# The second norm's normalising, turns, projection and residual addition two steps sooner in the memory stage

## The reference, cut to what matters

```python
keys = (x @ Wk.T + bk).reshape(B, L, N_QUAT, 4)
keys = keys / jnp.maximum(knorm, NORM_EPS)
values = (x @ Wv.T + bv).reshape(B, L, N_QUAT, 4)
bound = quat_mul(values, keys)
memory = jnp.cumsum(bound, axis=1)
retrieved = quat_mul(memory, quat_conj(keys)).reshape(B, L, D)
retrieved = retrieved / jnp.sqrt(positions)[None, :, None]
normed = (retrieved - mu) / jnp.sqrt(var + LN_EPS) * ln_g + ln_b
return x + (normed @ Wo.T + bo)
```

## Time and profile before

| | us |
|---|---|
| median of three runs | 881.63 |
| profiled execution | 886.1 |
| its span, first to last instruction | 884.3 |
| PE busy | 759.0 (86%) |
| DVE busy | 639.8 (72%) |
| ACT busy | 463.6 (52%) |
| POOL busy | 479.7 (54%) |
| mean granted PE clock | 0.919 |

### The profile page before, as it was taken

One profiled execution on the slowest core, in us unless ns is written; L12 is line 12 of the kernel. 1 busy time (PEld: TensorE's weight loads), 2 busy tenths in 40 slices (PEclk: granted clock), 3 DMA queues, 4 the chain that ended last, 5 costly groups with the idle time before them and its releaser, 6 DMA issues.

```text
span 884.3 us, 14563 instructions
## 1 busy us (share of the span) xinstructions
PE 759.0 (86%) x3937; PEld 572.3 (65%) x3938; DVE 639.8 (72%) x1468; ACT 463.6 (52%) x927; POOL 479.7 (54%) x438
## 2 busy tenths in 40 slices
PE   5999999996488299943989997998989898989997
PEld 2444444553377299942878886777868686868785
DVE  3789999988364255534699996878786968787864
ACT  2455556652122177723466655665656565756553
POOL 2677777765036444432356663554655555555554
PEclk9999999998555599975899999899999999999999
DMA  5000000000392122211000003545546281909280
GB/s 184 0 1 1 0 1 0 0 2 0 47 371 93 45 62 64 69 39 48 18 20 1 1 1 82 114 99 109 121 85 146 60 171 37 189 23 193 49 165 12
DMA packets 36383, 60.14 MB, mean 68 GB/s; under 512 B 3568, under 2 KB 15472, under 8 KB 35680
## 3 DMA queue, kind: packets, MB, share of 16 engines
q1 hardware_dynamic: 34048, 54.73, 26.6%
q0 software_dynamic: 2272, 4.67, 1.6%
HBM read 51.11 MB, written 8.28 MB: 67 GB/s over the span
## 4 chain that ended last, share of the span: by engine, by line
PE 31%; issue 8%; POOL 7%; DVE 6%; ACT 2%; DMA 1%; POOLq 0%; SPq 0%; DVEq 0%; ACTq 0%
PE c_m L1496 3%; PE c_m L1498 3%; PE c_m L1497 3%; POOL d_hid_lo L2017 2%; PE c_v L1496 1%; PE c_k L1496 1%; PE c_o L1550 1%; PE c_k L1497 1%; PE c_k L1498 1%; POOL c_bound L1984 1%; PE c_o L1547 1%; PE c_o L1548 1%; POOL c_read L1990 1%; PE c_v L1498 1%; PE c_r L1550 1%
## 5 line engine op out<-in xcount | busy, mean ns | idle before, releaser
L2017 POOL TENSOR_TENSOR d_hid_lo<-c_bound,d_hid_hi 128x512 fp32r<-128x512 f32 x136 | 176.6, 1299 | 152.6 <-ACT d_hid_hi L1947 152.4
L1947 ACT ACTIVATE d_hid_hi<-c_bound 128x512 fp32r<-128x512 f32 x136 | 85.2, 626 | 49.8 <-DVE c_bound L1809 48.8
L576 POOL TENSOR_TENSOR a_rs<-a_r,a_state 128x512 f32<-128x512 f32 x64 | 75.2, 1186 | 29.9 <-DVE a_state L419 27.5
L419 DVE TENSOR_TENSOR_SCAN a_state<-a_decay,a_state,a_vb 128x512 f32<-128x512 f32 x64 | 81.2, 1269 | 0.0
L1076 POOL DMA_INDIRECT results<-b_y_row,b_result_row x39 | 37.5, 960 | 51.9 <-DVE b_y_row L999 35.3
L1496 PE MATMUL c_m<-d_x_hi,d_hi 128*128 128x512 f32 x136 | 56.3, 414 | 7.5 <-DVE c_bound L1809 7.5
L1800 DVE TENSOR_TENSOR c_m<-c_bound,c_m 128x512 f32<-128x512 f32 x64 | 44.3, 692 | 23.7 <-PE c_m L1498 17.4
L1800 DVE TENSOR_TENSOR c_v<-c_bound,c_v 128x512 f32<-128x512 f32 x64 | 44.3, 692 | 22.2 <-PE c_v L1498 16.7
L990 DVE TENSOR_TENSOR b_hidden<-b_h,b_b 128x512 f32<-128x512 f32 x39 | 27.0, 692 | 42.9 <-PE b_h L826 42.2
L1498 PE MATMUL c_m<-d_x_hi,d_lo 128*128 128x512 f32 x136 | 54.1, 398 | 0.0
L1497 PE MATMUL c_m<-d_x_lo,d_hi 128*128 128x512 f32 x136 | 54.1, 398 | 0.0
(11 more groups left out here) (305 smaller groups left out, 2181.2 us busy)
## 6 DMA issues: line engine op xcount, KB each, us to landing
d_w_wide<-pair_weights SPq DMA_DIRECT2D x64, 512.0 KB, 12.1
b_w<-in_w SPq DMA_DIRECT2D x2, 2048.0 KB
d_w_wide<-in_moe SPq DMA_DIRECT2D x3, 1088.0 KB
b_xin<-rows_in SPq DMA_DIRECT2D x39, 64.5 KB
d_w_wide<-results SPq DMA_DIRECT2D x8, 256.0 KB
out<-c_read SPq DMA_DIRECT2D x8, 256.0 KB, 2.2
a_weights<-in_mixing SPq DMA_DIRECT2D x1, 901.0 KB
shape_consts<-in_consts SPq DMA_DIRECT2D x1, 744.0 KB, 5.0
```

Source lines behind the costliest of these rows:

```text
L419: dve.tensor_tensor_scan(state[:, j, seq_cols(h, 1)], decay[:, h, :], vb[j % 3][:, :], first, ALU.mult, ALU.add).then_inc(scan_ready, 1)
L576: pool.tensor_tensor(rs[:, j, :], rr[:, h, :], state[:, j, seq_cols(h, 0)], ALU.mult).then_inc(rs_ready, 1)
L1947: act.activation(hid_hi[:, n % HALVES, :], hidden[:, r, :], ACT.Copy).then_inc(hi_ready, 1)
L2017: pool.tensor_tensor(hid_lo[:, n % HALVES, :], hidden[:, r, :], hid_hi[:, n % HALVES, :].bitcast(F32), ALU.subtract).then_inc(lo_ready, 1)
```

## The change

In the tail, ACT's two halves of the normalising go from steps 6 and 7 to 4 and 5 and `normed_t` from 9 to 7; PE's turns go from step 8 to 6 and the projection from 11 to 9; DVE's addition goes from step 13 to 11. Within a step the tail comes first, so in step 4 ACT meets the normalising and its wait for `shift2` before copy 1, and in step 11 DVE meets the addition before `lo`. No instruction is added, dropped or altered, and POOL's and SP's orders stay.

```diff
                 def tail(i, h, step):
-                    if step == 8:
+                    if step == 6:
                         pe.wait_ge(normed_ready, i + 1)
...
-                    if step == 11:
+                    if step == 9:
                         pe.wait_ge(normedt_ready, i + 1)
                         need(pe, x_ready, i)
                         project(bank_o, "bo", "wo", normed_t).then_inc(wo_out, 1)
...
-                    if step == 13:
+                    if step == 11:
                         dve.wait_ge(wo_out, i + 1)
                         dve.wait_ge(kept_ready, i + 1)
...
-                    if step in (6, 7):
-                        if step == 6:
+                    if step in (4, 5):
+                        if step == 4:
                             act.wait_ge(shift2_ready, i + 1)
                             need(act, normedt_out, i)
-                        for s in (0, 1) if step == 6 else (2, 3):
+                        for s in (0, 1) if step == 4 else (2, 3):
...
-                        if step == 7:
+                        if step == 5:
                             a.then_inc(normed_ready, 1)
-                    if step == 9:
+                    if step == 7:
                         act.wait_ge(normedt_out, i + 1)
                         need(act, wo_out, i)
```

## The result

The changed kernel takes 892.26 us (median of 4 runs, 891.38 to 892.57) against 880.63 us (879.02 to 881.84): 1.32% slower, ratio 1.0132 with the 95% interval 1.011 to 1.0153. Forecast was 891.9.

The account below looks back on a forecast made before the run. DVE and PE were taken as both nearly full in a memory-stage body of 14.9 us. Terms 0.9 + 6.5 + 2.06 + 1.70 - 0.88 gave +10.3 on 881.6: 891.9 us, range 885 to 895.5.

Parts of the forecast that it names:

- `normed` can't start sooner: On ACT, normed already starts 0.04 us after shift2 ends, so standing sooner in the order can't start it sooner.
- Bodies 1 to 6: Memory-stage delays from got to got: body 1 +0.9 us, bodies 2 to 5 +1.63 each, body 6 +2.06.
- Copy 3 at Z+4.07: ACT's last memory copy ends 4.07 us after Z, shift2's end: 1.52 us later than before, bounds 0.98 and 2.1.
- `memory_n` +0.77: DVE's memory_n, which had 0.75 us of slack, starts 0.77 us later, 4.11 us after shift2 ends.
- first sum +0.41: PE's first sum of read comes 0.41 us later, 5.26 us after shift2 ends.
- `got` at Z+10.74: DVE's got starts 10.74 us after shift2 ends, not 9.11: +1.63 us a body.
- The port: DVE and GpSimd instructions exclude each other, first issued first; lo now waits for GpSimd's second read, delaying real and got.
- Rival 1: Port waits don't grow, second lo precedes GpSimd's second bound: +0.5 us a body, +4.5 in all, 886.1 us; chance 0.24.
- The gain of the projection on PE costs nothing: The projection, 1.43 us on PE, moves into a stretch where PE would wait for read: costed at nothing.
- Body 7, +1.70: Tile 0's routing: exponentials on ACT start 1.70 us later, behind normed and copy 1.
- rival 4: PE's clock falls once more, with a pause ahead of the first memory sum: +13.7 us, 895.3; chance 0.07.
- The last tail in the units, -0.88: In the experts' first tile, the last tail's normed moves ahead of a Silu that DVE waited for: -0.88 us.

Follow-up runs that it names:

- run 10: The changed kernel with ACT's last pair of key parts in step 8, behind memory copy 3, in place of step 7: 895.74 us, ratio 1.0105.
- run 1: The changed kernel with only DVE's residual addition back at step 13: 885.33 us, ratio 1.0046.
- run 2: The kernel before with only DVE's residual addition moved from step 13 to 11: 883.97 us, ratio 1.004.
- run 8: The changed kernel with the last lo piece moved from step 15 of body 6 to step 13 of body 7, behind the routing: 894.23 us, ratio 1.0114.
- run 3: The kernel before with GpSimd's kept issued in step 0, behind its two bound products, in place of step 4: 880.16 us, ratio 0.9995.
- run 7: The changed kernel with the tail of tile 6, in body 7, on its old steps on ACT, PE and DVE: 893.85 us, ratio 1.0084.
- run 11: As run 6, with the last lo piece behind the routing and ACT's last key parts behind copy 3: 884.45 us, ratio 0.9979.
- run 6: The changed kernel with DVE's addition at step 13, GpSimd's kept in step 0 and body 7's tail on its old steps: 884.82 us, ratio 1.0000.
- run 9: The changed kernel with body 7's tail on its old steps and the last lo piece behind the routing: 891.89 us, ratio 1.0068.

## Why the prediction was right, and where it was not

- *`normed` can't start sooner*: right; 0.03 us behind `shift2`, as before.
- *The whole, 891.9 against 892.26*: nearer than the mechanism was known. The base came out 1.0 us lower than the one used (880.63, not 881.6) and the difference 1.3 higher (11.6, not 10.3), and these two cancel by luck. Bodies 1 to 6 are no luck: +9.5 of +9.5 forecast, with each step below.
- *Copy 3 at Z+4.07*: 4.08. But I put it down to ACT's queue with PE keeping up by Z+3.8; run 10 showed PE at Z+3.70, so the two tie. The 0.98 us I gave as a lower bound of the delay was no bound of use: the true one is some 0.1 below 1.52.
- *`memory_n` +0.77, first sum +0.41, `got` at Z+10.74*: 4.12, 5.41 and 10.76; the first sum 0.15 later than forecast, off the path.
- *The port*: `lo` ends at 7.70 (forecast 7.68), `real` 9.12 (9.09), second `lo` 10.83 (10.81). Runs 1 and 2 show this term by itself: 1.02 us with ACT's order, 0.87 without. Rival 1, which gave the second `lo` the port first, fell: bodies of about the size it gave (15.55) came only when the addition was back. That the first to ask runs first held in every body looked at.
- *The gain of the projection on PE costs nothing*: right; PE now waits 0.23 us for `read`.
- *Body 7, +1.70*: this failed in its size: +2.87. The order's part was right to 0.01 us (run 8). Missing was PE's pause of 2.42 us ahead of the body and the low clock behind it, which I held as rival 4 with the price of one 6.7 us stretch; it came as 3.4 us, and cost 1.2. That rival was held at 0.07, on the reading that the clock fell behind full in one stretch. It was wrong: the profile of the kernel before has the clock low in others too, up to about 30 us into the memory stage. Its row, in 40 slices of 22.1 us, tenths of the full clock:

```profile
PEclk9999999998555599975899999899999999999999
```

- *The last tail in the units, -0.88*: failed in its sum, +0.1. The first half of `normed` did move, from 10.8 us behind the first product that waits for the weights to 6.6 us behind it; that it gained its 0.88 us is not shown. PE ran at 1.2 GHz for 10.2 us behind the transfer, not 6.8. Sorted by that length over all runs, the time from the first waiting product to the end is:

| low clock behind the transfer | tail at its old steps | two steps sooner |
|---|---|---|
| 3.4 us | | 332.1, 332.3, 332.4, 332.3, 332.3 |
| 6.8 us | 333.3, 333.3 | 331.8, 331.7 |
| 10.2 us | 334.0 | 333.4, 333.1, 333.3 |

At equal length the kernels with the tail two steps sooner are 0.6 to 1.5 us shorter there, which takes in the forecast 0.88; but they differ in other things too (run 2, in the left column, has its addition sooner). (The first line isn't the lowest, so that length isn't all that differs.)

Two misses, +1.6 in body 7 with the transfer and +1.0 in the units, make the trace's 12.9 against 10.3. Against the medians, 11.6 and 10.3, a part of that is one execution's scatter. What decides how long the clock stays low behind the transfer is open: it was 3.4, 6.8 or 10.2 us with nothing changed there. Open too is what brings the late falls in body 7: PE had the same pause of 0.87 us ahead of the output projection in runs 2, 3, 7 and 11, which fell, and in the kernel before and runs 6 and 9, which did not.

## What to carry to other kernels

Before moving a step sooner, ask what it waits for: if it already starts when its input comes, moving it can only put its wait ahead of others, and each instruction that it passes on a full engine is then behind that wait. On two engines that exclude each other at a port, the place of an instruction that needs no port matters too: 0.68 us moved by three places made two others lose 1.2 us. Where PE's clock can fall, a pause saved or added in front of a critical stretch can be worth more than its length: from run 7 to run 9 the pause got 1.4 us shorter, body 6 1.4 us and body 7 another 2.3. It need not be: from the changed kernel to run 8 the same pause gave body 6's 1.4 us and nothing in body 7.

## What the runs showed of the hardware

- GpSimd products and DVE instructions with both inputs in SBUF went one after the other, by order of asking, in all bodies read, though the program has no semaphore between them: `shift2` on four numbers a partition 0.17 us free and 1.23 behind `kept`; `lo` 0.72, 1.20, 1.32 or 1.78 by its place alone. Not every GpSimd instruction does this: an addition with both inputs in SBUF ran its usual 0.69 us beside GpSimd's power, here in the kernel before:

```profile
485.55 1.01 POOL L2000 TENSOR_TENSOR c_rstd<-c_var_eps,c_minus_half 128x4 f32<-128x4 f32 x1
485.67 0.69 DVE L1593 TENSOR_TENSOR x_tok<-x_tok,d_w_wide 128x512 f32<-128x512 f32 x1
```

- A pause of PE of 2.42 or 2.43 us ahead of body 7 was followed within 0.9 us by 3.4 us at half clock in four kernels of four; one of 0.99 to 1.69 us was not in nine of nine. Falls behind shorter pauses came all the same, in some kernels and not in others.
